# The delta-rule scan with its key products stored by token, and x3's first norm four operations sooner

## The reference, cut to what matters

```
def step(Sm, inp):
    qi, ki, vi, bi = inp
    Sk = jnp.einsum('bhkv,bhk->bhv', Sm, ki)
    upd = ki[..., :, None] * (vi - Sk)[..., None, :]
    Sm = Sm + bi[..., None, None] * upd
    oi = jnp.einsum('bhkv,bhk->bhv', Sm, qi)
    return (Sm, oi)
...
h = hidden_states + o @ Wo
y = rmsnorm(h, ln2)
h = h + jax.nn.silu(y @ Wg) * (y @ Wu) @ Wd
...
x = _layernorm(x + _L1_attn_ref(...), axis=-1)          # this is x3
x = _layernorm(x + _L1_ffn_ref(x, ...), axis=-1)        # this is x4, the output
```

## Time and profile before

| | us |
|---|---|
| median of 3 runs (lowest to highest) | 1350.47 (1347.79 to 1351.57) |
| the profiled execution | 1351.84 |
| its span | 1349.7 |
| PE busy | 1164.6 (86%) |
| DVE busy | 910.4 (67%) |
| ACT busy | 643.7 (48%) |
| POOL busy | 473.0 (35%) |

### The profile page before, as it was taken

The page is one execution under the profiler, slowest core; times in us unless marked ns, Lnnn a source line. Parts: engine busy times, 40 slices in busy tenths (PEclk is TensorE's granted clock), DMA queues, the critical chain, the costliest instruction groups (busy, mean ns, idle before and its releaser), DMA issues.

```text
span 1349.7 us, 19203 instructions
## 1 busy us (share of the span) xinstructions
PE 1164.6 (86%) x6118; PEld 616.3 (46%) x6118; DVE 910.4 (67%) x2097; ACT 643.7 (48%) x1258; POOL 473.0 (35%) x594
## 2 busy tenths in 40 slices
PE   5989889999898999999989581158899999999997
PEld 3434346454463554535535340124355455455553
DVE  3536535556577678686765776898888988988231
ACT  2061753745737537356365330314446745745642
POOL 3031220311323233143323136245356456466410
PEclk8989998999999999999989895578899999999999
DMA  3212030130311423314111239320220220200000
GB/s 100 83 48 71 1 110 9 46 98 34 110 41 29 139 64 81 94 33 143 39 44 42 58 70 239 97 50 9 49 58 16 58 57 16 57 24 8 24 9 8
DMA packets 85747, 79.83 MB, mean 59 GB/s; under 512 B 42800, under 2 KB 63408, under 8 KB 83632
## 3 DMA queue, kind: packets, MB, share of 16 engines
q1 hardware_dynamic: 85680, 79.01, 21.7%
HBM read 43.17 MB, written 35.00 MB: 58 GB/s over the span
## 4 chain that ended last, share of the span: by engine, by line
PE 60%; DVE 17%; ACT 10%; issue 7%; POOL 3%; DMA 2%; SPq 1%; ACTq 0%; DVEq 0%; POOLq 0%
PE ps L1318 14%; PE ps L1299 7%; PE ps L965 5%; PE ps L934 4%; PE ps L1002 4%; ACT arena L1451 4%; ACT arena L1413 3%; PE ps L968 3%; DVE arena L1850 3%; PE ps L975 3%; PE ps L1309 3%; PE ps L991 2%; PE ps L1069 2%; PE ps L1061 2%; PE ps L1051 2%
## 5 line engine op out<-in xcount | busy, mean ns | idle before, releaser
L1850 DVE TENSOR_REDUCE arena<-ps 128x4 f32<-128x512 f32 (+2 forms) x192 | 197.7, 1043 | 90.3 <-PE ps L968 87.4
L1318 PE MATMUL ps<-arena,late 128*128 128x512 f32 x512 | 227.0, 595 | 0.3 <-ACT arena L1600 0.3
L1413 ACT ACTIVATE arena<-ps 128x512 f32<-128x512 f32 (+2 forms) x200 | 109.7, 566 | 232.1 <-PE ps L934 105.6
L756 POOL TENSOR_SCALAR_AFFINE_SELECT arena<-arena 128x512 f32<-128x512 f32 x128 | 83.8, 657 | 295.1 <-ACT arena L1451 293.8
L1451 ACT ACTIVATE arena<-ps 128x1024 f32<-128x1024 f32 (+3 forms) x256 | 169.8, 711 | 33.3 <-PE ps L991 32.0
L1318 PEld LDWEIGHTS ps<-arena,late 128*128 128x128 f32 x512 | 96.3, 192 | 114.3 <-issue 112.0
L975 PE MATMUL ps<-mask_qk,ident_b 128*128 128x512 bf16 x450 | 124.2, 391 | 27.3 <-DVE arena L2134 26.1
L1600 ACT ACTIVATE arena<-ps,f_s 128x512 f32<-128x512 f32 x128 | 83.3, 688 | 109.4 <-PE ps L1318 98.5
L1413 ACT ACTIVATE arena<-ps,arena 128x128 f32<-128x128 f32 (+1 forms) x128 | 62.3, 529 | 125.1 <-DVE arena L1877 51.9
L934 PE MATMUL ps<-ident,arena 128*128 128x128 f32 (+1 forms) x624 | 99.2, 291 | 22.8 <-ACT arena L1413 13.1
L1299 PE MATMUL ps<-arena,late 128*128 128x512 f32 x256 | 115.6, 604 | 2.1 <-ACT arena L1600 2.1
(11 more groups left out here) (187 smaller groups left out, 1969.2 us busy)
## 6 DMA issues: line engine op xcount, KB each, us to landing
qr<-q_rep SPq DMA_DIRECT2D x8, 1024.0 KB, 5.6
kr<-k_rep SPq DMA_DIRECT2D x8, 1024.0 KB, 8.0
scan_d<-late SPq DMA_DIRECT2D x56, 138.0 KB, 3.0
arena<-scan_d SPq DMA_DIRECT2D x12, 552.0 KB, 6.8
q_rep<-hilo SPq DMA_DIRECT2D x24, 256.0 KB, 3.3
k_rep<-hilo SPq DMA_DIRECT2D x24, 256.0 KB, 3.9
proj_d<-arena SPq DMA_DIRECT2D x8, 768.0 KB, 5.1
late<-proj_d SPq DMA_DIRECT2D x8, 768.0 KB, 4.5
```

The costliest lines, as they stand in the source:

```text
L756: g.affine_select(out=block, in_=block, compare_op=ALU.is_ge, fill=0.0, base=0, pattern=[[0, 4], [1, P]], channel_multiplier=-1).then_inc( ...
L1318: last = pe.matmul(ps[:, ring2.bank(f"{n}{c}"), :], w[:, k, c * P:(c + 1) * P], src[:, k, :], start=(k == 0), stop=(k == HC - 1))
L1413: return act.activation(dst, src(ps[:, bank, :]), func, **kw)
L1850: v.tensor_reduce(heads[:, 2 * pr:2 * pr + 2, gs[0]:gs[-1] + 1], ps[:, at:at + 2, 0:len(gs) * w].rearrange("p q (n w) -> p q n w", w=w), X ...
```

## The change

A chunk of k_u is now 5 rows of 64 words: a row of 64 products for each of the 4 tokens, and the old state as the fifth row. The state is now 64 words side by side. Line 2114 and the copy on ScalarE (line 1658) read it so, and the sum writes it so. For that, the product of u and the keys runs over token, value, key element. It reads u repeated 8 times, and the keys with a distance of 64 words from one element to the next; before, it read 4 words side by side. The sum over the 5 rows reads with a distance of 64 words from one word to the next; before, it read 320 words side by side. Instructions and elements are as many as before. In the changed kernel the product is line 2122 and the sum line 2129.

Second, AT_X goes from 58 to 54: in step 1, norm_x3 starts behind 54 of the scan's operations.

```
-        k_u = [c2.take(QUARTER * HD, HD, CH + 1) for _ in range(2)]
-        live = [tile[:, :, :, CH].rearrange("p (c v) d -> p c v d", v=HD) for tile in k_u]
+        k_u = [c2.take(QUARTER * (CH + 1), HD, HD) for _ in range(2)]
+        live = [tile.rearrange("p (c j) v d -> p c j v d", j=CH + 1)[:, :, CH] for tile in k_u]
...
-                    yield o.mark(v.tensor_tensor(k_u[half][:, rows, :, 0:CH], now_u.unsqueeze(2).broadcast_to([P, HD, HD, CH]),
-                                                 kt[:, c, :, :].unsqueeze(1).broadcast_to([P, HD, HD, CH]), ALU.mult))
+                    first = at * (CH + 1)
+                    yield o.mark(v.tensor_tensor(k_u[half][:, first:first + CH, :, :],
+                                                 now_u.rearrange("p v j -> p j v").unsqueeze(3).broadcast_to([P, CH, HD, HD]),
+                                                 kt[:, c, :, :].rearrange("p d j -> p j d").unsqueeze(2)
+                                                 .broadcast_to([P, CH, HD, HD]), ALU.mult))
...
-                    yield o.mark(v.tensor_reduce(after[:, (c + 1) % QUARTER, :, :], k_u[half][:, rows, :, :], X, ALU.add))
+                    yield o.mark(v.tensor_reduce(after[:, (c + 1) % QUARTER, :, :],
+                                                 k_u[half][:, first:first + CH + 1, :, :].rearrange("p j v d -> p v d j"), X, ALU.add))
...
-AT_Y, AT_H_FIRST, AT_H, AT_X, AT_S, AT_FIRST = 4, 21, 26, 58, 60, 44
+AT_Y, AT_H_FIRST, AT_H, AT_X, AT_S, AT_FIRST = 4, 21, 26, 54, 60, 44
```

## The result

| | before | changed |
|---|---|---|
| median of 13 runs, us | 1350.47 | 1358.04 |
| lowest to highest, us | 1346.19 to 1357.42 | 1353.45 to 1363.25 |
| the profiled execution, us | 1351.84 | 1358.11 |
| its span, us | 1349.7 | 1354.8 |

The ratio is 1.0056, with a 95% interval of 1.0039 to 1.0072: the change makes the kernel slower by 7.6 us. The forecast was 1361.7.

A forecast was written before the change was run, and what follows sets the result against it. VectorE's scan bounds first, later PE with VectorE nearly full. Terms +3.6 +2.7 -2.1 +0.2 +1.1 +5.7 = +11.2 us on 1351.84 give 1363.0, as a median 1361.7; range 1344 to 1368, the forecast's own 1358 to 1364.

The forecast's parts named there:

- step 2: VectorE's waits of 2.23 and 3.33 us absorb 15 chunks' growth; only the scan's last chunk counts, +0.2 us.
- steps 4 to 7: VectorE's work grows from 48.84 to 52.44 us against 51.01, so PE waits: +1.43 us each, 5.7 together.
- The cheap read bought once and paid for twice: In each scan chunk: line 2114 -196 ns, product +197, sum +224; net +225 ns, 3.6 us a scan.
- The reason given for the sum's price: The sum's five rows are nearer to the many places that don't fit than to two: 0.70 ns an element.
- Steps 0 and 1: All 16 chunks on the chain, +3.6 us; then chunks up to the norm, +2.7; the norm's earlier start, -2.1.
- Step 3: The scan's growth of 3.6 us less a wait of 1.68 and slack of 0.83: +1.1 us.
- What would show it: Line 2114 about 420 ns, product 620, sum 710; GpSimd wait gone, line 1633 waiting for line 2158's norm, step 52.4 us.
- A: The sum reads its five rows at full rate; a chunk costs +1 ns, total 1347.3 us, not slower; chance 0.30.
- B: The product's read of the keys is free as well; a chunk falls by 195 ns, total 1342.5 us; chance 0.10.
- C: The sum's reads cost half the price, about 110 ns; total 1351 us, no change; chance 0.06.
- D: Product's and sum's reads cost 1.0 ns like ScalarE's strided copy; a chunk +0.38 us, total 1379 us; chance 0.07.

The follow-up runs named there:

- second pair of traces: Both kernels traced again, unchanged; from the scan's first instruction to line 1633 at the end of step 7 the change costs 7.2 us, 4.6 in the first pair.
- experiment 3: Changed kernel with the keys stored token by token, so the product reads 8 key elements side by side; ratio 0.9979 to the kernel before, median 1348.74 us.
- Experiments 4 to 8: Kernel before with other k_u groupings, norm at 54; sum reads 2, 8, 4, 16, 32 words apart and takes 486, 731, 742, 706, 712 ns.
- Experiment 9: Changed kernel with AT_H at 22 in place of 26, h's norm one chunk sooner; ratio 1.0047 to the kernel before.
- experiment 4: Kernel before with k_u and keys in pairs of key elements, 10 words a group, norm at 54; ratio 0.9939, median 1340.53 us.

## Why the prediction was right

The direction and the mechanism held, and most sizes. The measured change, 7.6 us, is two thirds of the forecast's 11.2, and 1358.0 lies at the lower edge of the forecast's own range. Nearly all of the gap is the chunk: with the measured 192 ns in place of 225, the prediction's own steps give 3.1 + 2.3 - 2.1 + 0.2 + 0.6 + 4 x 0.9 = 7.7 us. That this meets 7.6 so well is partly luck, since step 2 came out 0.7 us above its term and steps 4 to 7 together 1.3 below theirs (second pair of traces). By its steps:

- **The cheap read bought once and paid for twice.** Right. Line 2114: -199 ns for the -196 forecast. The sum: +221 for +224. The product: +170 for +197, and experiment 3 shows that the whole of it is the keys' read. A chunk came to +192 ns, not +225.
- **The reason given for the sum's price** was wrong where its size was right. I put it down to five places being nearer to line 2114's eight than to line 1971's two or three, with no word on the distance. Experiments 4 to 8 show that five places are free 2 words apart and dear from 4 words on. So the 0.70 ns was a choice between two rows that happened to be near the 0.69 measured.
- **Steps 0 and 1.** With 192 ns the prediction's own terms give 16 x 0.192 = 3.1, 13 x 0.192 - 0.199 = 2.3 and -2.1: 3.3 us, and both pairs of traces show 3.1. fo was there in time: PE ends it at 926.5 in the changed kernel and the norm starts at 928.4.
- **Step 2** was put at +0.2 and came to +0.9 in the second pair. In that pair the granted clock from 950 to 960 was 0.83 before and 0.66 with the change. Nothing that I ran separates the clock from the scan there; it stays open.
- **Step 3:** 3.07 - 1.68 - 0.83 = 0.6 by the prediction's terms, 0.8 measured.
- **Steps 4 to 7** is the term that was mis-sized: forecast 1.43 us each, measured 0.5 to 0.6. With the measured chunk it should be 48.84 + 3.07 - 51.01 = 0.9. The remainder is in line 1770, which follows the norm's statistics: it takes 0.50 us while GpSimd works on line 851 and 853 beside it, and 0.17 us in the changed kernel, where VectorE comes to it later and GpSimd has stopped. Over one step (1037.11 to 1088.12 before, 1040.92 to 1092.42 changed) every other group of VectorE outside the chunk takes the same time within 0.02 us, so the dense work grows by 3.07 - 0.33 = 2.74 us, from 48.84 to 51.6; the traces have 51.5. The row of before is this one, from its timeline:

```profile
1038.73 0.50 DVE L1770 TENSOR_TENSOR slot_T<-arena 128x4 f32<-128x4 f32 x1
```

That GpSimd is the cause is read from the two timelines; no experiment moved it alone.

- **What would show it.** The wait for GpSimd went, as said. That line 1633 would wait for x3's norm in each step was wrong: ScalarE's queue still held it back in steps 3 to 7 (no idle time before it at 1045.95), and most of PE's wait came at h's norm. Experiment 9 shows that this is a matter of place only: with h's norm sooner, line 1633 does wait for line 2158 (0.62 us at 1043.18).
- **The rivals.** A (the sum at full rate) falls with 709 ns; its condition is what experiment 4 provides by another layout. B's time, 1342.5, is close to what experiment 4 has, 1340.5, which is all four instructions at the full rate; B's 6.7 us for steps 0 and 1 were 6.3 there, and the norm did wait for fo (1.0 us), as B has it. C falls too: the sum's reads cost 221 ns and not 110. D falls: no read of the changed kernel cost 1.0 ns an element.

## What to carry to other kernels

When a layout makes one strided read contiguous, list every reader and writer of the data with the distance in its innermost dimension, and price each: here one of three VectorE accesses got cheap and two dear, and on the bound engine 192 ns a chunk became 7.6 us. Before giving up such a change, look for a grouping in which every access takes neighbouring words, at least in pairs, or steps by no more than 2 words; interleaving in pairs had it for all four instructions, and was 0.6% faster than the start. When two engines are both nearly full, work out the dense time of each in a step (the period less its waits): that, and not the place where a wait shows, says which one sets the pace.

## What the runs showed of the hardware that was not expected

- A VectorE sum over single-precision words in SBUF takes the same time for reads 1 and 2 words apart (488 and 486 ns for 320 words), and 0.7 to 0.8 ns more for each word from 4 words apart on: 742 and 731 ns at 4 and 8, 706 to 712 at 16, 32 and 64. All are sums over five places; 3 words apart wasn't run.
- Yet a product that goes in turn over 2 or 3 places 16 words apart ran at 0 and 0.07 ns over the full rate, and a sum over five places 16 words apart didn't (706 ns). What makes the first cheap wasn't tried.
- Writes with gaps (runs of 4 words in every 5 and of 8 in every 9), and one PSUM element read 8 times in a row, cost nothing (419 and 422 ns for 256 products). ScalarE's copy of 256 words fell from 668 to 413 ns when its reads went from 5 words apart to runs.
- TensorE's granted clock fell in one execution and not in another of the same kernel, and that step differed by 3.4 us, 2.4 of them in one group of 16 products.
